# One PE order for a linear-attention kernel: another start, and the state products of a chunk moved directly behind the heads

## The reference

```
xn = layernorm(x)
q, k, v = heads(xn @ Wq.T), heads(xn @ Wk.T), heads(xn @ Wv.T)
q, k divided by the largest row norm of their head
num = cumsum(v) + q . cumsum(k (x) v)        # over the tokens of a batch
den = arange(1, n + 1) + q . cumsum(k)
attn = (num / den) @ Wo.T + bo
top 2 of softmax(xn @ router_w), weights renormalised
ffn = sum over both of  weight * (silu(xn @ gate[e]) * (xn @ up[e])) @ down[e]
out = x + attn + ffn
```

## Time and profile before

| | us |
|---|---|
| median of 3 runs | 1373.83 (1367.58 to 1375.96) |
| the profiled execution | 1375.33 |
| its span, first to last instruction | 1373.6 |
| PE busy in the span | 1242.6 (90%) |
| DVE, ACT, POOL busy | 932.9, 708.5, 368.6 |
| mean granted clock of TensorE | 0.963 of full speed |

### The profile page before, as it was taken

The page is one execution under the profiler, slowest core; times in us unless marked ns, Lnnn a source line. Parts: engine busy times, 40 slices in busy tenths (PEclk is TensorE's granted clock), DMA queues, the critical chain, the costliest instruction groups (busy, mean ns, idle before and its releaser), DMA issues.

```text
span 1373.6 us, 59302 instructions
## 1 busy us (share of the span) xinstructions
PE 1242.6 (90%) x23920; PEld 1087.7 (79%) x23921; DVE 932.9 (68%) x2662; ACT 708.5 (52%) x1683; POOL 368.6 (27%) x605
## 2 busy tenths in 40 slices
PE   6689999998999999999999999999689999999960
PEld 5468878887887788888788888878579999999960
DVE  6567768776876777787687778667365555555532
ACT  4355656646665654666566466555244444444430
POOL 5300112121111111112111211213523555555546
PEclk9799999999999999999999999999789999999995
DMA  6000000000000000000000000020121222222218
GB/s 212 26 3 6 11 11 17 9 13 13 12 13 10 16 9 13 13 11 13 11 15 10 15 11 11 15 95 18 35 62 52 62 62 61 61 61 62 61 59 348
DMA packets 36324, 55.56 MB, mean 40 GB/s; under 512 B 7600, under 2 KB 26544, under 8 KB 35856
## 3 DMA queue, kind: packets, MB, share of 16 engines
q1 hardware_dynamic: 25744, 29.02, 7.0%
q0 software_dynamic: 9216, 19.17, 4.1%
q10 hardware_dynamic: 1152, 4.19, 0.7%
HBM read 28.33 MB, written 24.02 MB: 38 GB/s over the span
## 4 chain that ended last, share of the span: by engine, by line
PE 70%; DVE 17%; issue 6%; POOL 2%; DMA 2%; ACT 1%; another core or an unknown queue 1%; POOLq 0%; SPq 0%; DVEq 0%; ACTq 0%
PE bank L1142 9%; PE bank L1143 8%; PE bank L1144 8%; PE bank L1312 7%; PE bank L1418 6%; PE bank L1240 6%; PE bank L1292 5%; PE bank L1277 4%; PE bank L1266 3%; PE bank L1179 3%; PE bank L1226 3%; PE bank L1411 3%; PE bank L1302 3%; DVE qs L778 2%; DVE num L849 2%
## 5 line engine op out<-in xcount | busy, mean ns | idle before, releaser
L473 POOL COPY xn<-meta 128x2 f32<-128x2 f32 x128 | 24.9, 195 | 748.6 <-PE bank L1277 747.3
L530 POOL DMA_INDIRECT expert_rows<-yt,wdi x136 | 132.0, 971 | 142.7 <-ACT yt L700 104.3
L575 ACT ACTIVATE kn<-bank 128x512 f32<-128x512 f32 x128 | 69.5, 595 | 192.9 <-PE bank L1226 171.4
L1142 PE MATMUL bank<-xTh,Wh 128*128 128x256 f32 x512 | 154.6, 302 | 2.2 <-DVE xs L772 1.5
L1144 PE MATMUL bank<-xTl,Wh 128*128 128x256 f32 x512 | 147.6, 288 | 5.5 <-issue 5.5
L1143 PE MATMUL bank<-xTh,Wl 128*128 128x256 f32 x512 | 147.4, 288 | 2.1 <-issue 1.8
L593 ACT ACTIVATE qs<-qs,cvec 128x128 f32<-128x128 f32 x480 | 146.1, 395 | 0.7 <-DVE cvec L824 0.2
L1142 PEld LDWEIGHTS bank<-xTh,Wh 128*128 128x128 f32 x512 | 100.4, 196 | 53.0 <-issue 45.6
L1312 PEld LDWEIGHTS bank<-WoT,numT 128*128 128x128 f32 x1024 | 123.1, 193 | 16.1 <-issue 11.7
L477 POOL DMA_INDIRECT sorted_tokens<-xn,slot x128 | 123.4, 964 | 40.5 <-POOL xn L473 29.1
L1312 PE MATMUL bank<-WoT,numT 128*128 128x128 f32 x1024 | 128.8, 279 | 0.8 <-ACT numT L586 0.8
(11 more groups left out here) (214 smaller groups left out, 3024.7 us busy)
## 6 DMA issues: line engine op xcount, KB each, us to landing
xt<-sorted_tokens SPq DMA_DIRECT2D x137, 66.0 KB
er<-expert_rows SPq DMA_DIRECT2D x16, 512.0 KB, 8.3
xa<-in_x SPq DMA_DIRECT2D x8, 512.0 KB, 11.6
out<-ot ACTq DMA_DIRECT2D x8, 512.0 KB, 6.6
gu<-in_gate_up_w SPq DMA_DIRECT2D x1, 2816.0 KB, 11.1
expert_rows<-yt,wdi POOLq DMA_INDIRECT x136
sorted_tokens<-xn,slot POOLq DMA_INDIRECT x128
wraw<-in_wkq SPq DMA_DIRECT2D x2, 512.0 KB, 5.7
```

The costliest lines, as they stand in the source:

```text
L530: pool.indirect_dma_start(ys_d, bass.IndirectOffsetOnAxis(ap=wdi[:, r:r + 1], axis=0), yt[:, r, :], None).then_inc(f_sc[r], 16)
L1142: pe.matmul(dst, ah, bh, start=start, stop=False)
```

## The change

Five things change, all in the order or number of instructions; the computed values are the same.

1. **Start.** ACT alternates the parts of Wh with the first `x_hi`. `wvraw` gets a place of its own.
2. **sums(b)** uses `wvraw` itself (two matmuls) and not `Wvh`, `Wvl` (four). `sums(0)` moves from behind the last fill into the third pair (`j == 2`), and with it DVE's `values_before(0)`, the constants and `values_parts(0)`.
3. **outer(g + 1)** on PE and **state(g + 1)** on DVE stand directly behind the heads in steps 0 to 6.
4. **Routing.** `choose` is cut in two, the second half at the end of step 2; `place_rows` moves from step 2 to 3 and the scatters one step on. In step 7 DVE copies the fills before it takes the norms' maximum.
5. The **blank blocks** have 16 rows, and there are 10 instead of 16.

The diff, cut to its core:

```diff
+        def landed(r):
+
+            return 1 if r < RT - 2 else 2
...
-            for n in range(2):
-                for r in range(RT):
+            for r in range(RT):
+                for n in range(landed(r)):
...
-                pool.indirect_dma_start(ys_d, IndirectOffsetOnAxis(ap=dump[:, r:r + 1], axis=0), blank[:, 0, 0:D], ...
+                pool.indirect_dma_start(ys_d, IndirectOffsetOnAxis(ap=dump[0:16, r:r + 1], axis=0), blank[0:16, 0, 0:D], ...

             act.preload_act_table(ACT.Sqrt)
-            act.wait_ge(w_in[0], 16)
-            for n in range(2):
+            def weights_hi(n):
+                act.wait_ge(w_in[n // 2], 16)
                 act.activation(Wh[:, 512 * n:512 * n + 512], wraw[:, 512 * n:512 * n + 512], ACT.Copy).then_inc(s_wh, 1)
+
+            weights_hi(0)
             batch_root(0)
+            weights_hi(1)
             for g in range(4):
                 normalise(g)
-            act.wait_ge(w_in[1], 16)
-            for n in range(2, 4):
-                act.activation(Wh[:, 512 * n:512 * n + 512], wraw[:, 512 * n:512 * n + 512], ACT.Copy).then_inc(s_wh, 1)
+            x_hi(0)
+            weights_hi(2)
+            x_hi(1)
+            weights_hi(3)
             act.wait_ge(w_in[2], 16)
             act.activation(rwh[:], rwf[:], ACT.Copy).then_inc(s_wh, 1)
-            x_hi(0)
-            x_hi(1)
...
+                if j == 1:
+                    dve.wait_ge(s_late, 9)
+                    values_before(0)
                 if j > 0:
                     norm_max(j - 1, 1)
...
                 norm_max(j, 0)
                 if j == 2:
+                    dve.wait_ge(s_late, 9)
+                    dve.wait_ge(s_const, 15)
...
+                    dve.wait_ge(s_chain, links[0])
+                    values_parts(0)
                     batch_scale(1)
-            dve.wait_ge(s_late, 9)
-            dve.wait_ge(s_const, 15)
...
-            values_before(0)
-            values_parts(0)
             norm_max(3, 1)
...
                 if c == CB - 1 and more:
-                    norm_max(G, 0)
                     for f in range(4, 8):
                         copy_fill(G, f)
+                    norm_max(G, 0)
...
+                if g + 1 < C:
+                    state(g + 1)
                 if c in (0, 2, 4) and more:
                     x_lo(G)
...
                 if c > 0:
                     attended(g - 1)
-                if g + 1 < C:
-                    state(g + 1)
...
                     if c == 1:
-                        choose(b)
+                        choose_first(b)
+                    if c == 2:
+                        choose_second()

...
             def sums(b):
...
-                for n, w in enumerate((Wvh, Wvl)):
-                    for par in range(2):
-                        last = pe.matmul(pbank("VC", b)[halves(par), :], xsr, w[:, 512 * par:512 * par + 512], ...
+                for par in range(2):
+                    last = pe.matmul(pbank("VC", b)[halves(par), :], xsr, wvraw[:, 512 * par:512 * par + 512], ...
...
+                if g + 1 < C:
+                    outer(g + 1)
                 if c in (0, 2, 4) and more:
                     transpose_x(G)
                 if g + 2 < C:
                     values(g + 2)
...
                 if c > 0:
                     project(g - 1)
-                if g + 1 < C:
-                    outer(g + 1)
```

More of the change, by code:

```diff
@@ L103, in build @@
         xTh, xTl = place("xTh", [P, NCP, 2, P], f32r), place("xTl", [P, NCP, 2, P], f32r)
-        at[0] += 4 * 4 * NCP * P - 512
+        wvraw = place("wvraw", [P, H * DH])
+        at[0] += 4 * 3 * NCP * P - 2560
         Wvh, Wvl = place("Wvh", [P, H * DH], f32r), place("Wvl", [P, H * DH], f32r)
@@ L297, in psum_order @@
                     continue
+                if g + 1 < C:
+                    yield from uses_D(g + 1)
                 if c in (0, 2, 4) and more:
@@ L862, in state @@
                             dve.wait_ge(z_tail, 16)
-                            for t_ in f_sc:
-                                dve.wait_ge(t_, 32)
+                            for r in range(RT):
+                                dve.wait_ge(f_sc[r], 16 * landed(r))
                             dve.tensor_copy(new, d).then_inc(e_st, 1)
@@ L890, in first_of, with choose_first @@
                                        slf[:, 0].unsqueeze(2).broadcast_to(bc), ALU.is_equal))
-            def choose(b):
+            def choose_first(b):
                 if b == 0:
@@ L1002, in _ @@
                 if j == 2:
[L1003 to L1020 removed]
+                    dve.wait_ge(s_late, 9)
+                    dve.wait_ge(s_const, 15)
+                    for n in range(2):
+                        links[0] += 1
+                        dve.tensor_copy(causal[halves(n), :], tri[halves(n), halves(n)]).then_inc(s_chain, 1)
+                    links[0] += 1
+                    dve.tensor_scalar(cntf[DH:P, 0:1], cntf[DH:P, 0:1], -float(DH * DH), None, ALU.add).then_inc(s_chain, 1)
+                    links[0] += 1
+                    dve.tensor_scalar(cntf[:, 1:2], negf[:, 0:1], 1.0, None, ALU.add).then_inc(s_chain, 1)
+                    dve.wait_ge(s_chain, links[0])
+                    link(dve.tensor_tensor(cntf[:, 0:1], cntf[:, 0:1], cntf[:, 1:2], ALU.mult))
+                    for n in range(2):
+                        links[0] += 1
+                        dve.tensor_copy(VC[:, n, :, DH], cntf[:, 0:1].broadcast_to([P, HP])).then_inc(s_chain, 1)
+                    dve.wait_ge(s_chain, links[0])
+                    values_parts(0)
+                    batch_scale(1)
             norm_max(3, 1)
@@ L1193, in sums @@
                 wait_bank(pe, "VC", b)
+                if b == 0:
+                    pe.wait_ge(w_in[3], 16)
                 pe.wait_ge(e_xsr, b + 1)
-                for n, w in enumerate((Wvh, Wvl)):
-                    for par in range(2):
-                        last = pe.matmul(pbank("VC", b)[halves(par), :], xsr[:].rearrange("p a s -> p (a s)"),
-                                         w[:, 512 * par:512 * par + 512].bitcast(f32), start=(n == 0), stop=(n == 1),
-                                         tile_position=(0, DH * par))
+                for par in range(2):
+                    last = pe.matmul(pbank("VC", b)[halves(par), :], xsr[:].rearrange("p a s -> p (a s)"),
+                                     wvraw[:, 512 * par:512 * par + 512], start=True, stop=True, tile_position=(0, DH * par))
                 last.then_inc(a_vc, 1)
@@ L1323, in _ @@
                     transpose_x(j + 2)
+                if j == 2:
+                    sums(0)
                 if j > 0:
```

28 lines of the change are left out of this document (14 added, 14 removed).

## The result

The changed kernel takes 1460.19 us (median of 4 runs, 1458.11 to 1462.07), against 1373.93 before; the ratio is 1.0638, with a 95% interval of 1.0606 to 1.0671. That is 86 us slower, where I forecast no change, and far outside the range. Of all executions in this document one, 1824.42 us with the 128-row blank blocks, was in a slow state (granted clock 0.642); it is left out.

A forecast was written before the change was run, and what follows sets the result against it. PE was taken to set the pace. Terms −7.6 − 6.5 − 4.5 − 2.2 − 8.5 + 5 + 28.5 − 3 = +1.2 on 1375.33 gave 1376.5 us profiled, 1375 as a median; range 1348 to 1391.

The forecast's parts named there:

- the sentence on routing: Routing: the scatters, moved a step later, are POOL's work that no PE wait names; no cost was entered for them.
- The sign that I had named for being right: PE's waits, 84 to 960 us: state products' wait on issue grows from 3.2 to 25 us or more.
- Instruction fetch, +28.5: Heads and D form one run of 400 instructions; page stops of 1.2 us, net +28.5 us, bounds 12 and 45.
- Rival A: Heads and D: page edges stay hidden in the contiguous run too, so 28.5 falls away: 1347 us; chance 0.2.
- Rival B: Heads and D: late page requests make a stop 1.9 us and not 1.2: 1392 us; chance 0.15.
- The last batch, −3: Last batch: D no longer stands in the halts behind the second blank-block burst: −3 us, 4 either way for scatters.
- Start, −7.6: Start, until the first scores at 80.31 us: all its parts together gain 7.6 us, bounds −3 and −15.
- (a): Start: one Wh cast leaves the first scale's way; PE's 1.51 us wait falls to about 0.3: −1.2 us.
- (b): Start: ten small blank-block issues in place of 16 shorten PE's slow stretch from 38.83 us: −9 us.
- (c): Start, third pair: DVE's constants and values_parts(0) delay the squares; PE waits 5.8 us more, low clock adds 2.3.
- D's own waits, −8.5: D behind the heads: its waits on num in step 2 (5.4 us) and in step 0 (3.2) go: −8.5 us.
- place_rows, +5: Routing: place_rows in step 3 delays squares and numT, +1.0 us a batch, less 0.28 for step 2: +5 us.

The follow-up runs named there:

- products back: Changed kernel with the state products and DVE's state put back ahead of keys, as in the kernel before: 1348.26 us, 0.9841.
- after, released behind scores: Changed kernel with POOL's scatters released when PE ends the step's last scores (keys in step 6; step 7 and last batch unchanged): 1392.00 us, 1.0128.
- both: Changed kernel with the state products back ahead of keys and POOL's scatters released behind the scores: 1347.06 us, 0.9828.
- its three variants: Kernel before with, in turn, state products directly behind the heads (1454.88 us), scatters released behind keys (1432.15), scatters released behind scores (1373.00).

## Why the prediction was wrong

Heads' starts in us, in the profiled executions:

| | before | after | products back | after, released behind scores | both |
|---|---|---|---|---|---|
| first heads | 84.4 | 75.4 | 76.2 | 75.9 | 74.6 |
| second batch | 203.8 | 197.3 | 191.8 | 195.6 | 189.8 |
| last batch | 919.4 | 991.6 | 900.9 | 920.8 | 897.4 |
| last chunk | 1017.7 | 1105.5 | 992.8 | 1038.3 | 988.7 |

**The step that failed** is the sentence on routing, "The scatters, a step later, are POOL's and no PE wait names them", together with its place in the sum: nothing. The prediction had read from the trace that indirect DMAs of POOL halt PE, had priced the two large bursts, and did not ask what the 112 single scatters of the first seven batches do. Their cover was the 3.5 us of values and project between the heads and D, and the move took exactly that cover away. The 32 products and 25 loads of that stretch were named, but only as time in which a page can arrive. The price: 68 us between the two releases with D behind the heads (D takes 3.5 us and not 1.1 in most steps, and the clock fell to half with 14 of them), against 1 with D further back. The sign that I had named for being right, a wait on issue of 25 us or more, came true at 45.1 us, but mostly for this other reason: it can't tell a page from a scatter, and 95 short stops can.

**Instruction fetch, +28.5.** Right in kind and near in size: with the scatters out of D's way 22.9 us in six batches by the count, 24.3 by the heads' starts of seven, 0.88 us a stop and not 1.2, in more stops than I had (26). In the changed kernel itself it is 15.2. Rival A is refuted: long products between the bursts took 20 us off. The Trainium skill's rule beside it ("Runtime: NRT & Kernel Launch", section "Instruction fetch mechanics", the crossing mostly hidden) holds here where long products stand between the bursts (0.6 us in D), and not inside such a run (22.9). Rival B, slower by fetch alone, was not it either.

**The last batch, −3.** Wrong in sign: 98.3 us before, 113.9 after, 91.9 with the products back. D's move costs 22 there in the changed kernel and 5 in the kernel before (103.5); I take it for the same scatters and pages, but no run parts them in this batch.

**Start, −7.6.** Right: −8.9 at the first scores (80.31 to 71.43) and the same at the first heads; first fill 11.59, forecast 11.9. The terms hold too. At the norms ahead of the third pair's chain PE is 9.6 ahead (54.57 to 44.94), forecast 10.2 for (a) and (b). At the last norms of the fourth pair 3.7 are left (65.57 to 61.84), so (c) cost 5.9, forecast 8.1. From there to the first scores it gains 5.2, forecast 5.5. But (c) came about otherwise than I had it: not one wait of 5.8 us for the squares but 1.52 there (2.98 with the products back) and, before it, 2.53 for the sums' bank, a wait that the prediction didn't have; the rest I take for half clock.

**Sums, −6.5.** Right: with the products back step 6 is 14.08 us (median of seven batches), before 14.95, so 0.87 a batch. **Squares, −4.5:** 8.5 to 3.3, so −5.2. **ks, −2.2:** wrong, the wait is still 2.2 with the products back.

**D's own waits, −8.5:** half right. The 5.4 on num do go with D's move, but choose cut removes them without it; the 3.2 on issue don't go (4.1 with the products back). **place_rows, +5:** with the products back and the scatters behind the scores, step 3 takes 13.48 us (13.64 before) and step 4 14.69 (14.15), so 0.4 a batch by medians, 3 in all; but step 2 is 1.9 a batch shorter (16.04 to 14.16), and the routing as a whole gains 10.

**Not foreseen:** step 7 of the seventh batch takes 22.6 to 24.7 us in all ten kernels of the changed line, wherever D stands, and 18.1 in the kernel before and its three variants. Most of it is one stop of PE and the half clock that comes with it. In the one with the products back:

```profile
891.47 0.56 PE L1255 MATMUL bank<-qs,ks 64*64 64x64 f32 x21
895.68 1.54 PE L1255 MATMUL bank<-qs,ks 64*64 64x64 f32 x43 [3.65 <-issue]
```

It ends 9.3 us after SP issues the load of the experts' weights (2816 KB) at 886.36. The clock falls to half within the stop and stays so for some 7 us. In the kernel before a stop of 1.42 us ends 10.7 us after the same load, and the clock stays. I take both for pages that come behind the weights; that is argued, no run tried it.

Without fetch, D's waits and the last batch the prediction's terms make −7.6 − 6.5 − 4.5 − 2.2 + 5 = −15.8; the kernel with the products back measured −21. These were sound in sum. The error is in one term that stood at nothing, the scatters, and in the last batch.

## What to carry to other kernels

When instructions move, look at what other engines are doing in the new place, not only at what they wait for there: an engine that no wait names can still slow this one, and the time it was harmless in was a cover. Mark the bursts of short instructions on PE and keep indirect DMAs of POOL, and each other, away from them; in this kernel the 400 instructions of some 10 ns each in one run needed long products between them. If a mechanism has been read from a trace in one place, list all places where its cause occurs before pricing any.

## What the hardware showed

Two indirect scatters of 128 rows, 1.44 us apart, hold PE to a handful of products per 0.75 us for about 2.3 us, beginning some 0.7 us after POOL's copy behind the release. Under the values and project (0.23 and 0.12 us a product) nothing of it shows: they take 172.4 us in six batches of the kernel before, with the scatters under them, and 171.7 with the scatters released behind the scores. Nor does it under the fills (144.3 and 142.9). The norms, 0.13 us a product, do show it when they stand right behind halted scores: 1.81 us for 1.07. Under products of 0.017 us it made 1.1 to 2.4 us a step. Shifting POOL's release by 5 us, with PE's program unchanged, cost 62 us (1.0457). The number of rows in a blank block made no difference that shows. A page's edge inside 400 short instructions cost 0.88 us on average. With D behind the heads the granted clock fell to 0.50 in 15 places, for 3 to 7 us each, 25 us in six batches. Single stops of D of up to 1.7 us, in the kernel released behind the scores, were followed by no fall.
